# Fusion attention in one softmax pass over 1500 keys, and context rows stored for 128 partitions

## The reference, cut to what matters

```python
memory_proj = einsum('bme,de->bmd', memory, W_mem)          # memory: 16 x 1500 x 128
scores = einsum('bnd,bmd->bnm', hidden_states, memory_proj) / sqrt(256)
attn = softmax(scores, axis=-1)                             # over 1500 keys, no mask
memory_context = einsum('bnm,bmd->bnd', attn, memory_proj)
gate = sigmoid(einsum('bnf,df->bnd', concat([hidden_states, memory_context]), W_gate) + b_gate)
x = rmsnorm(hidden_states + gate * memory_context)
```

## Time and profile before

| what | us |
|---|---|
| median of 3 runs | 1562.52 (1562.12 to 1567.64) |
| the profiled execution, its own time | 1564.41 |
| its span in the trace | 1562.6 |
| PE busy in the span | 1470.6 (94%) |
| DVE, ACT, POOL busy | 939.1, 621.7, 561.0 |

### The profile page before, as it was taken

One profiled execution on the slowest core, in us unless ns is written; L12 is line 12 of the kernel. 1 busy time (PEld: TensorE's weight loads), 2 busy tenths in 40 slices (PEclk: granted clock), 3 DMA queues, 4 the chain that ended last, 5 costly groups with the idle time before them and its releaser, 6 DMA issues.

```text
span 1562.6 us, 21954 instructions
## 1 busy us (share of the span) xinstructions
PE 1470.6 (94%) x8042; PEld 779.7 (50%) x8043; DVE 939.1 (60%) x1605; ACT 621.7 (40%) x1014; POOL 561.0 (36%) x425
## 2 busy tenths in 40 slices
PE   6879999999999889989998999999999989999898
PEld 3446555555555444446664345555344345555344
DVE  6887666666666254213336768887442768888440
ACT  1253566666666520025542334443122334344131
POOL 1620588888888820000000134452000125444000
PEclk9989999999999999989999989999999999999999
DMA  7001533232332140013311001110030101110000
GB/s 259 1 5 42 141 88 77 73 99 60 91 75 56 31 141 0 0 40 120 114 38 66 1 19 43 37 38 13 2 115 27 40 13 38 48 37 13 3 1 23
DMA packets 42276, 82.96 MB, mean 53 GB/s; under 512 B 6252, under 2 KB 28188, under 8 KB 42156
## 3 DMA queue, kind: packets, MB, share of 16 engines
q1 hardware_dynamic: 42160, 81.48, 17.9%
HBM read 59.31 MB, written 0.97 MB: 39 GB/s over the span
## 4 chain that ended last, share of the span: by engine, by line
PE 85%; DVE 8%; POOL 2%; ACT 2%; issue 2%; DMA 0%; SPq 0%; POOLq 0%; ACTq 0%; DVEq 0%
PE psum L1820 22%; PE psum L2403 10%; PE psum L2061 5%; PE psum L2037 5%; PE psum L2011 4%; PE psum L2344 3%; PE psum L1994 3%; PE psum L2375 3%; PE psum L2211 3%; PE psum L2395 3%; PE psum L1980 2%; PE psum L2398 2%; PE psum L2396 2%; PE psum L2397 2%; DVE WA L1463 2%
## 5 line engine op out<-in xcount | busy, mean ns | idle before, releaser
L1463 DVE TENSOR_REDUCE WA<-psum 112x2 f32<-112x1000 f32 x192 | 229.9, 1201 | 89.9 <-PE psum L2011 89.9
L780 POOL TENSOR_TENSOR XN<-XN,WBZ 125x896 f32<-125x896 f32 x128 | 266.4, 2082 | 16.8 <-POOL XN L780 0.9
L1174 ACT ACTIVATE WA<-psum,y_bias 125x448 f32<-125x448 f32 x192 | 121.0, 633 | 202.9 <-PE psum L2398 201.8
L1008 ACT ACTIVATE WBZ<-psum 125x896 f32<-125x896 f32 x192 | 175.5, 915 | 43.9 <-PE psum L2037 33.7
L2403 PE MATMUL psum<-WA,ctxN 125*128 125x448 f32 x384 | 179.5, 551 | 0.4 <-ACT WA L1174 0.4
L812 POOL TENSOR_TENSOR XN<-const,y_max 112x896 bf16<-112x896 f32 x32 | 75.2, 2350 | 263.9 <-DVE y_max L1710 191.6
L1710 DVE CUSTOM_DVE_ANT_0 XA<-psum,WA 112x375 bf16<-112x375 f32 x240 | 125.4, 542 | 47.1 <-PE psum L2375 46.0
L803 POOL TENSOR_SCALAR ctxT<-ctxT 128x375 f32<-128x375 f32 x32 | 56.1, 1754 | 189.7 <-ACT std L881 187.1
L2037 PE MATMUL psum<-R 100*125 100x224 f16 x768 | 110.7, 266 | 0.0
L1723 DVE RECIPROCAL WBZ<-WBZ 128x224 f32<-128x224 f32 x68 | 105.0, 1546 | 0.1
L2037 PEld LDWEIGHTS psum<-R 100*125 100x125 f16 x768 | 78.9, 135 | 28.3 <-issue 25.0
(11 more groups left out here) (266 smaller groups left out, 2555.7 us busy)
## 6 DMA issues: line engine op xcount, KB each, us to landing
R<-WA SPq DMA_DIRECT2D x192, 93.8 KB, 2.2
ctxT<-in_ctxT SPq DMA_DIRECT2D x12, 750.0 KB, 4.2
R<-in_ctxT SPq DMA_DIRECT2D x12, 750.0 KB, 5.5
WA<-in_ctxT SPq DMA_DIRECT2D x8, 750.0 KB, 4.2
ctxT<-in_ctxT SPq DMA_DIRECT2D x32, 187.5 KB
ctxN<-in_ctx SPq DMA_DIRECT2D x32, 187.5 KB
WBZ<-in_x_w SPq DMA_DIRECT2D x4, 1024.0 KB, 6.4
WA<-bias_rows SPq DMA_DIRECT2D x30, 82.0 KB, 3.6
```

What stands on the lines that cost most here:

```text
L780: nc.gpsimd.tensor_tensor(z_sum[b % 2][0:TK, :], first[0:TK, :], z_p[t % 4][0:TK, :], ALU.add)\
L1008: nc.scalar.activation(z_p[t % 4][0:TK, :].rearrange("p (k n) -> p k n", k=2), psum[0:TK, s:s + 2, 0:2 * GC], ACT.Exp, scale=float(CHD0) * ...
L1174: nc.scalar.activation(y_pT[t][0:TK, g * HALF:(g + 1) * HALF], bank[2 + u % 3][0:TK, 0:HALF], ACT.Exp, bias=y_bias[0:TK, bass.ds(b * NT + ...
L1463: V.tensor_reduce(z_mx[0:PR, r:r + 3:2, c], psum[0:PR, lo:lo + 2, 0:PC], AX_X, ALU.max)\
```

## The change

The fusion attention is written anew, unrolled over 8 walks.

- One set of scores of 1500 keys per walk, in four banks at once (`m_scored`, banks 0 to 3), one reduction over all of them (`m_maximum`, `AX_XY`), one exponential over 128x1500 with its sum (`m_exps`). There is no running maximum, no alpha and no rescaling.
- The probabilities are transposed in 12 pieces of 125 neighbouring keys, in three groups of four (`m_turned`), copied by ACT in groups of four, and the 12 products of a walk accumulate in one bank (`m_attended`). DVE divides (`m_divide`), PE transposes back (`m_back`), ACT writes XB. POOL has no part in it.
- The context rows are no longer transposed on the chip. They are loaded from DRAM, beside the columns, into three sets of buffers. One set lies in WA, where the next layer's attention weights stood by then. `attention_weights(0)` is issued after the last product of the attention.
- DRAM tensor `ctx` holds per sequence 128 partitions by 12x128 elements, where partitions 125 to 127 are zeros. Layers 2 and 3 load their rows of a chunk from it as 128 partitions by 1536 bytes, with a row pitch of 6144 bytes.

The diff, cut to its core (the removed `attention` functions are those described above):

```diff
             def chunk(b, c, slot, name):
                 load(ctxT[slot][:, :], a["ctxT"][:, bass.ds(b * NK + c * CK, CK)], name)
-                load(ctxN[slot][0:TK, :, :].rearrange("p t c -> p (t c)"),
-                     a["ctx"][bass.ds((b * CHUNKS + c) * TK, TK), :], name)
+                load(ctxN[slot][:, :, :].rearrange("p t c -> p (t c)"),
+                     a["ctx"][bass.ds(b * P, P), bass.ds(c * (KT * C), KT * C)], name)
...
+            def m_columns(i):
+                for j in range(2):
+                    b = 2 * i + j
+                    load(m_ctxT[i % 3][j], a["ctxT"][:, b * NK:(b + 1) * NK], f"m_columns{i % 3}")
+            def m_rows(i):
+                for j in range(2):
+                    b = 2 * i + j
+                    load(m_ctxN[i % 3][j].rearrange("k t x -> k (t x)"), a["ctx"][b * P:(b + 1) * P, :],
+                         f"m_rows{i % 3}")
+            sp.wait_ge(sem("z_pv"), NT * B)
+            for i in range(2):
+                m_columns(i)
+                m_rows(i)
+            emptied(sp, ("down", 1, 1))
+            m_columns(2)
+            m_rows(2)
+            sp.wait_ge(sem("m_scores"), 1)
+            m_columns(3)
+            for i in range(3, HB):
+                if i + 1 < HB:
+                    sp.wait_ge(sem("m_scores"), i - 1)
+                    m_columns(i + 1)
+                sp.wait_ge(sem("m_pv"), i - 2)
+                m_rows(i)
+            sp.wait_ge(sem("m_pv"), HB)
             attention_weights(0)
...
ACT
+            def m_exps(i):
+                act.wait_ge(sem("m_max"), i + 1)
+                if i > 1:
+                    act.wait_ge(sem("m_turned"), PARTS3 * (i - 1))
+                nc.scalar.activation(m_p[i % 2]..., m_scores, ACT.Exp,
+                                     bias=nmax_all[:, i % 2:i % 2 + 1], accum_out=lsum_all[:, i % 2:i % 2 + 1])
+            m_exps(0)
+            for i in range(HB):
+                m_turned(i, 0)
+                m_turned(i, 1)
+                if i + 1 < HB:
+                    m_exps(i + 1)
+                m_turned(i, 2)
+                if i > 0:
+                    m_back(i - 1)
+            m_back(HB - 1)
...
DVE
+            m_maximum(0)
+            for i in range(HB):
+                if i > 0:
+                    m_divide(i - 1)
+                if i + 1 < HB:
+                    m_maximum(i + 1)
+            m_divide(HB - 1)
...
PE
+            def m_scored(i):
+                pe.wait_ge(sem(f"m_columns{i % 3}"), 32 * (i // 3 + 1))
+                if i > 0:
+                    pe.wait_ge(sem("m_exp"), i)
+                for u in range(CHUNKS):
+                    for j in range(2):
+                        at = i * PR + j * S
+                        mm = pe.matmul(bank[u][QP * j:QP * (j + 1), 0:CK], m_flat[:, at:at + QP],
+                                       m_ctxT[i % 3][j][:, u * CK:(u + 1) * CK], start=True, stop=True)
+            def m_turned(i, g):
...
+                for k in range(4):
+                    t = 4 * g + k
+                    mm = pe.transpose(bank[4 + n % 2][0:TK, k * P:(k + 1) * P], m_p[i % 2][:, t * TK:(t + 1) * TK], ident)
...
+            m_scored(0)
+            for i in range(HB):
+                if i + 1 < HB:
+                    m_scored(i + 1)
+                m_turned(i, 0)
+                m_turned(i, 1)
+                if i > 0:
+                    m_back(i - 1)
+                m_attended(i, 0)
+                m_turned(i, 2)
+                m_attended(i, 1)
+                m_attended(i, 2)
+            m_back(HB - 1)
+            pe.wait_ge(sem("m_kept"), HB)
```

More of the change, by code:

```diff
@@ L293, in build @@
                       .rearrange("p (b h s) -> p b h s", b=B, h=4) for t in (XB, XN))
-        cmax, nnew, ddec, alpha, rsum = (sb(n, [P, 4]) for n in ("cmax", "nnew", "ddec", "alpha", "rsum"))
+        cmax = sb("cmax", [P, 4])
         QH = HEADS * S
@@ L393, in take @@
             return bank[bk]
-        FOURS = 2 * NT // 4
         LANDED = 16 * 2
[L400 to L403, removed]
         def entry(eng, col, hi, lo=0):
             return eng.value_load(table[0:1, bass.ds(col, 1)], min_val=lo, max_val=hi)
[L408 to L449, removed]
         def ahead(b, t):
@@ L704, in _ @@
                 stage_keys(i)
[L706 to L745, removed]
             def divide(b):
@@ L1049, in _ @@
             evacuate(B - 1)
[L1051 to L1084, removed]
-                    act.wait_ge(sem("x1_pv"), CHUNKS * (b - 1) + 2 if not isinstance(b, int) or b > 0 else 2)
-                    j, t = f // (FOURS // 2), f % (FOURS // 2) * 4
-                    nc.scalar.activation(m_ctxN[p][j][0:TK, t:t + 4, :],
-                                         bank[3][0:TK, :].rearrange("p (t c) -> p t c", t=4), ACT.Copy)\
-                        .then_inc(sem("m_rows"), 1)
-                def main(b, p, e0, i, word):
-                    more = not c["masked"] and not (isinstance(b, int) and b == N - 1)
-                    for u in range(U - 1):
-                        exps(e0, u + 1)
-                        if more:
-                            rows_of_context(b + 1, 1 - p, 2 * u)
-                        turn(e0, u)
-                        if more:
-                            rows_of_context(b + 1, 1 - p, 2 * u + 1)
-                def tail(b, p, e0, i):
-                    turn(e0, U - 1)
-                def finish(b, p):
-                    for r in range(rounds):
-                        act.wait_ge(sem(x + "_oT"), (l * N + b) * rounds + r + 1 + 2 * rounds)
-                        w = per * M
-                        dst, src = R[:, bass.ds(b * HEADS * S + r * w, w)], bank[2 + r][:, 0:w]
-                        if n == 1:
-                            dst = XB[:, 0, bass.ds(b * PR, PR)].rearrange("p (j s) -> p j s", j=2)
-                            src = src.rearrange("p (j q) -> p j q", j=2)[:, :, 0:S]
-                        nc.scalar.activation(dst, src, ACT.Copy).then_inc(sem(x + "_rows"), 1)
-                def begin(b, p):
-                    word = word_of(act, x, b, l, total)
-                    first(b, p, word[1], 0, word)
-                def attend(b, p, before, behind):
-                    walk(act, x, b, p, l, total, first, main, tail,
-                         lambda: begin(b + 1, 1 - p) if behind else None)
-                    if before:
-                        finish(b - 1, 1 - p)
-                if not c["masked"]:
-                    for f in range(FOURS):
-                        rows_of_context(0, 0, f)
-                over_walks(act, N, begin, attend)
-                finish(N - 1, 1)
@@ L1222, in _ @@
         def _(dve):
-            for x in CFG:
-                dve.sem_inc(sem(x + "_added"), 4)
             dve.sem_inc(sem("x2_rowmax"), 2)
@@ new lines, in m_back @@
+            def m_back(i):
+                pe.wait_ge(sem("m_normed"), i + 1)
+                mm = pe.transpose(bank[6 + i % 2][:, C:2 * C], m_o[i % 2], ident)
+                mm.then_inc(sem("m_back"), 1)
+            m_scored(0)
[10 more added lines that the diff above has]
+                m_attended(i, 2)
@@ L2515, in arrange @@
         "xT": c(x.reshape(T, D).T),
[L2516 removed]
+        "ctx": c(np.pad(ctxs.reshape(B, NT, TK, C).transpose(0, 2, 1, 3), ((0, 0), (0, P - TK), (0, 0), (0, 0)))).reshape(B * P, NT * C),
         "ctxT": c(ctxs.reshape(B * NK, C).T),
```

254 lines of the change are left out of this document (63 added, 191 removed).

## The result

The changed kernel takes 1501.0 us (median of 4 runs, 1497.8 to 1503.6) against 1564.1 for the kernel before in the same comparison: a ratio of 0.959, interval 0.957 to 0.962. The forecast was 1506, with a range of its own of 1499 to 1513, and up to 1518 with the longer chain. On two more occasions it measured 1503.3 and 1499.9, ratio 0.959 both times.

What follows compares the result with a forecast made beforehand. PE was taken to bound the kernel and its attention stage. The stage's 58.5 us saving less 2 for a low clock gave -56.5, from 1562.5 to 1506 us; range 1499 to 1513, extended to 1518 with the longer chain.

Steps and rivals of the forecast that it cites:

- the longer chain: Rival in the attention walk: wide operations cost as much as four small ones, or hand-overs more; 1515 us, chance 0.10.
- What bounds the kernel: Whole kernel and attention stage: PE sets the pace, busy 94% of the span and 113.9 of 128 us in the stage.
- Worth nothing by itself: Work removed from ACT, DVE and POOL in the stage: lay beside PE, no gain except waits already counted in 14.83 us.
- The walk: One walk of the attention stage: 8.1 us by the chain over DVE and ACT, against 14.83 before.
- lower bound: Walk limited by PE's own work, 7.5 us: 0.6 us less a walk, 4 in all.
- The sign that I had named: In each walk, PE waits a little for ACT's copy before the last values.
- The clock: Start of the new stage: low clock again for some us, costing 2 us, bounds 0 and 5.
- the rival: Clock stays at 1.2 GHz in the stage: 1559 us, or 1574 if it lasts through following products; chance 0.05.
- The loads: Context loads, 3.11 MB a walk at 378 GB/s, 8.2 us: hidden by slack of 11 to 16 us.
- Weights, layers 2 and 3: Next layer's weights moved behind the attention, 8.3 us, hidden; padded rows in layers 2 and 3 zero, bounds 0 and 1.
- a sign: The first product behind the attention stage starts 56 to 58 us earlier.
- the load-bound stage: Rival: loads of walks 2 to 7 run at 183 GB/s, stage ends 34 us later than forecast; 1540 us, chance 0.05.

Runs made afterwards that it cites:

- before, neighbouring columns: Kernel before, with its 36 transposes a walk reading 125 neighbouring columns instead of columns 3 apart: 1552.7 us, ratio 0.992.
- before, rows loaded: Kernel before, with context rows loaded from padded DRAM, neighbouring columns, two buffer sets and padded rows in layers 2 and 3, running softmax kept: 1506.3 us, ratio 0.963.
- one maximum, rows made on PE: Changed kernel, with context rows again made by 24 transposes a walk on PE and six ACT copies instead of loaded: 1537.2 us, ratio 0.982.
- four reads: Changed kernel, with the maximum by four reductions of 375 and one of 4, the exponential by four instructions of 375: 1513.2 us, ratio 0.967.
- the stride: Changed kernel, with its probabilities transposed from columns 3 elements apart instead of neighbouring ones: 1506.0 us, ratio 0.962.
- two sets: Changed kernel, with two sets of context buffers instead of three: 1501.1 us, ratio 0.960.

## Why the prediction was right

**What bounds the kernel: right.** The stage follows PE's work, and taking PE work out of it moved its end. Taking the stage in steps, each measured: neighbouring columns 13.2 us (127.9 to 114.7), loading the rows another 44.1 (to 70.6), one maximum another 4.8 (to 65.8). In the other order the maximum is worth 15.5 (114.7 to 99.2) and the rows 33.4. The last step also takes in what the change does besides (division on DVE, the third set of buffers, the moved weights); the third set alone is worth nothing.

PE's time in windows of 3 to 5 whole walks at clock 1.00 shows why the two orders differ (us a walk; the last column is the stage less seven walks):

| kernel | PE busy | PE idle | ends |
|---|---|---|---|
| before | 13.79 | 1.04 | 24.1 |
| before, neighbouring columns | 11.60 | 1.35 | 24.1 |
| before, rows loaded | 8.13 | 0.12 | 12.9 |
| one maximum, rows made on PE | 10.81 | 0.72 | 18.6 |
| changed | 7.34 | 0.23 | 12.8 |

PE's work adds up: the rows are 3.47 us a walk in either order and the maximum 0.79. What does not add up is the waiting and the start. Of the 10.7 us between 15.5 and 4.8, 5.3 lie in the walks (with the rows made on PE, the maximum also removes 0.63 us of waiting) and 5.4 at the ends, where the first walk's context transposes stood alone ahead of its scores, at the low clock; with one maximum they run behind the first scores at 1.00. The forecast's share of 4.7 us a walk for the context transposes was right in size: 3.47 for the rows, and about 1.5 of the 2.19 for the stride.

*"Worth nothing by itself"* was right for DVE, ACT and POOL: their small instructions lay beside PE. But the running softmax also cost PE 0.79 us a walk in smaller stretches of each product, which the forecast did not name as a gain; it lay hidden in its new sum.

**The walk: right to 0.5 us, and this is the mis-sized term.** Forecast 8.1 by the chain over DVE and ACT, measured 7.57, which is its lower bound: PE's own work, put at 7.5. Term by term, from the start of the scores:

- scores until the reduction starts: 2.9 forecast, 2.75 measured. I doubled a figure of two chunks that held a changeover; 16 records in a row take 2.53.
- reduction and its hand-overs: 1.82 forecast, 1.75 measured. The slope over elements was right (1.73 forecast, 1.72 measured), so four banks cost nothing over two that this trace shows.
- exponential: 1.58 forecast, 1.51 measured. The third copy starts 1.51 us behind its start, 0.1 us before the sum's read ends.
- third copy and hand-over: 0.71 forecast, 0.69 measured.
- last values: 1.08 forecast, 0.87 measured. They follow the second group's values without a changeover.

Seven walks by 0.53 make 3.7 us. The chain of waits names another loop, PE's own work with 0.77 us for the first copy in it (the second group of transposes lies beside that, so PE is idle for only 0.23), of the same length. The four reads and the stride each lengthen one loop and both lengthen the walk, so neither has slack to speak of. The sign that I had named, a wait of PE before the last values, did not come: the third copy is done 0.1 us before they start, and PE waits for the first copy instead. PE's 7.5 us were 7.34.

**The clock: right in size, uncertain in occurrence.** I took 2 us. It is 1.6 (67.4 against 65.8), and came in two of the three profiled executions of this kernel. The reading behind the rival was wrong in one point: the stretch at half clock did not hold transposes alone. The first scores stand in the second half of that window of the earlier trace rows and are at 0.50 too, and the two groups of transposes before 687 are at 1.00. In the timeline of the kernel before:

```profile
694.16 0.89 PE L2150 MATMUL psum<-ctxT,WBZ 128*64 128x375 f32 x1
```

**The loads: right that they hide, with a premise that I had not examined.** 378 GB/s was too low as a ceiling: the queue moved 401 to 423 at the start and 396 over 32 us with two sets. A walk of lead less costs nothing. The padding was the condition that I had set at 2% more bytes; I priced it only for layers 2 and 3, and took for granted in the fusion layer that a row load runs as fast as the loads in the earlier trace rows. It does, because of the padding. That this held was not reasoned, and without it the stage is 40 us longer.

**Weights, layers 2 and 3: right.** No wait on a load ahead of the first product, and the kernel behind the stage moved by 1.3 us, inside the scatter. Neither part was tried alone.

**The sum.** Forecast for the stage 69.4 and 2 for the clock, 56.5 us saved. Measured 62.1 without a clock loss: 3.7 us from the walks and 2 from the clock make up the 5.6 us between. So the product behind the stage came 63.2 us earlier (811.57 to 748.36), outside the 56 to 58 that I had named as a sign. The rivals did not occur. The longer chain happened in the experiment with four reads and cost 12 us, near the 9 of its bound; the load-bound stage happened with 125 partitions, where the stage was 40 us longer, against 34.

## What to carry to other kernels

Where a chain over several engines and one engine's own work come out alike, both set the pace, and each edit pays by the smaller of what it takes off the two; find which by lengthening one. A transformation made on the busiest engine is worth a load in its place while the queue has room, but only if the load is cut so that all DMA engines take part (128 partitions here, not 125). And when several edits go in together, take them out singly: here one, transposes of neighbouring columns instead of a stride of 3, was worth 13 us of the stage and could have been had without the rest.

## What the runs showed of the hardware that I had not expected

- In a group, transposes of 125 columns that stand 3 elements apart follow each other every 0.195 us, those of neighbouring columns every 0.11, and the weight load takes 256 to 260 ns against 187 to 191; in a walk of 36 this made 1.9 us, after waits.
- One DVE reduction over four PSUM banks takes 1.72 us for 1500 elements and one ACT exponential 1.51; split by bank, with the small reduction and four sums, they take 2.1 and 2.3.
- A load of 125 partitions ran at 132 GB/s with a DMA share of 0.32; loads of 128 partitions queued at up to 423, and at 396 over 32 us.
- With 3.5 us without PE work behind the first scores, the granted clock fell to 0.5 in two profiled executions and stayed at 1.00 in a third of the same kernel.
- The same scores, transposes and values kept PE busy for 8.13 us a walk in 11 stretches and for 7.34 us in 6.
